# Second attention of a decoder layer: when the value products, the projections and the copies are issued within a unit of sixteen steps

## The reference

```
q = _heads(x @ Wq + bq); k = _heads(x @ Wk + bk); v = _heads(x @ Wv + bv)      # 16 heads of 16
att = einsum('bhqd,bhkd->bhqk', q, k) * scale, -inf above the diagonal
y = einsum('bhqk,bhkd->bhqd', softmax(att), v)
qc = _heads(x @ Wcq + bcq); kc = _heads(cross_input @ Wck + bck); vc = _heads(cross_input @ Wcv + bcv)
attc = einsum('bhqd,bhkd->bhqk', qc, kc) * scale
y = y + einsum('bhqk,bhkd->bhqd', softmax(attc), vc)
return y @ Wp + bp
```

## Time and profile before

| | |
|---|---|
| time, median of 3 runs | 1344.24 us (1342.76 to 1344.56) |
| the profiled execution | 1347.11 us, its span 1345.4 us |
| PE busy in the span | 1190.8 us, 89% |
| DVE busy | 913.5 us, 68% |
| ACT busy | 830.3 us, 62% |
| POOL busy | 479.5 us, 36% |
| first maximum and last score of the second attention | 617.3 and 1018.2 us |

### The profile page before, as it was taken

One profiled execution on the slowest core, in us unless ns is written; L12 is line 12 of the kernel. 1 busy time (PEld: TensorE's weight loads), 2 busy tenths in 40 slices (PEclk: granted clock), 3 DMA queues, 4 the chain that ended last, 5 costly groups with the idle time before them and its releaser, 6 DMA issues. The chain is left out here.

```text
span 1345.4 us, 25018 instructions
## 1 busy us (share of the span) xinstructions
PE 1190.8 (89%) x8862; PEld 552.4 (41%) x8862; DVE 913.5 (68%) x2337; ACT 830.3 (62%) x1584; POOL 479.5 (36%) x511
## 2 busy tenths in 40 slices
PE   6699999999999999375888888888888369999998
PEld 2244444444444443261222232232224336666666
DVE  3777777777777777435788887878841755756564
ACT  3466666666666666450577777677773465666663
POOL 0267888877888888420112111111220000000000
PEclk9999999999999999696799999999997679999999
DMA  7544222222222221202121211212100082332100
GB/s 220 156 98 103 54 57 50 49 51 57 54 57 52 49 49 24 89 8 84 46 69 49 68 52 47 68 46 60 44 2 1 2 313 78 127 125 80 64 16 17
DMA packets 75954, 91.98 MB, mean 68 GB/s; under 512 B 12242, under 2 KB 67538, under 8 KB 75798
## 3 DMA queue, kind: packets, MB, share of 16 engines
q1 hardware_dynamic: 74806, 90.25, 23.9%
q0 software_dynamic: 1024, 0.13, 0.1%
HBM read 54.36 MB, written 10.68 MB: 48 GB/s over the span
## 5 line engine op out<-in xcount | busy, mean ns | idle before, releaser
L1023 DVE TENSOR_REDUCE a_mx<-a_m 128x1 f32<-128x512 f32 (+3 forms) x512 | 269.0, 584 | 74.6 <-PE a_m L829 62.8
L960 ACT ACTIVATE a_pt<-a_s 128x512 f32<-128x512 f32 (+3 forms) x512 | 235.5, 515 | 88.4 <-PE a_s L857 85.1
L449 ACT ACTIVATE a_pt<-a_s 128x512 f32<-128x512 f32 x256 | 149.4, 597 | 164.3 <-DVE a_s L544 135.8
L829 PE MATMUL a_m<-a_k,a_q 48*128 48x512 f16 (+3 forms) x512 | 131.0, 362 | 53.9 <-DVE a_mx L1023 44.2
L537 DVE CUSTOM_DVE_ANT_0 a_junk<-a_m,a_rtile 128x512 f16<-128x512 f32 x256 | 167.3, 687 | 2.0 <-issue 2.0
L604 POOL TENSOR_TENSOR a_ps<-a_ps,a_pt 128x512 f32<-128x512 f32 x128 | 159.9, 1272 | 1.4 <-ACT a_pt L449 1.4
L333 PE MATMUL a_o<-a_pt,a_v 128*64 128x512 f32 x512 | 139.0, 621 | 0.1
L829 PEld LDWEIGHTS a_m<-a_k,a_q 48*128 48x128 f16 x512 | 36.2, 94 | 202.1 <-DVE a_mx L1023 160.7
L870 PE MATMUL a_o<-a_pt,a_v 128*17 128x512 f32 (+3 forms) x1024 | 119.1, 538 | 0.0
L544 DVE TENSOR_TENSOR a_s<-a_s,a_near 128x218 f32<-128x218 f32 (+1 forms) x256 | 108.0, 433 | 15.5 <-PE a_s L324 12.9
L857 PE MATMUL a_s<-a_q,a_k 49*128 49x512 f16 (+3 forms) x512 | 114.4, 352 | 3.3 <-ACT a_pt L960 3.1
(11 more groups left out here) (208 smaller groups left out, 2430.8 us busy)
## 6 DMA issues: line engine op xcount, KB each, us to landing
a_q<-a_nat SPq DMA_DIRECT2D x192, 64.0 KB
a_k<-a_nat SPq DMA_DIRECT2D x192, 64.0 KB
ex_raw<-in_Wa SPq DMA_DIRECT2D x12, 1024.0 KB, 4.9
ex_raw<-in_Wb SPq DMA_DIRECT2D x12, 1024.0 KB, 7.1
halves<-a_natc SPq DMA_DIRECT2D x32, 128.0 KB, 2.4
halves<-a_nat SPq DMA_DIRECT2D x16, 256.0 KB, 2.1
a_q<-halves SPq DMA_DIRECT2D x32, 128.0 KB, 2.7
a_k<-halves SPq DMA_DIRECT2D x32, 128.0 KB, 2.8
```

The source lines that it names most:

```text
L449: act.activation(pt[:, n % RING, ::-1], bank_s[j % 2][:, :], ACT.Exp, scale=SC1 / QS).then_inc(sm["act_s"], 1)
L829: mm[h] = pe.matmul(bank_m[j % 3][:, 0:keys], q[u % 3][o:o + ROW_M, pair, x, qb * P:(qb + 1) * P], k[u % 3][o:o + ROW_M, pair, x, 0:keys], ...
L960: act.activation(pt[g % 4][:, h, first:], bank_s[(32 * u + j) % 3][:, first:], ACT.Exp, scale=SC2 / QS).then_inc(sm["act_s"], 1)
L1023: dve.tensor_reduce(mx[u % 2][:, qb, to:to + 1], bank_m[j % 3][:, 0:keys], AX.X, ALU.max).then_inc(sm["dve_b"], 1)
```

## The change

The table of steps changes in five places, and the two chunks of a projection are issued in one step instead of two. In steps of the period (all counted as above):

| | before | after |
|---|---|---|
| cross projection, PE | 4 and 5 | 4 |
| self projection, PE | 11 and 12 | 10 |
| high and low half of self, ACT and DVE | 12 and 13 | 11 and 12 |
| value products, PE | 10, 12, 14, 0, 2, 4, 6, 8 | 11, 13, 15, 1, 3, 5, 7, 9 |
| copies of `bank_o`, ACT | 1 and 9 | 2 and 10 |
| turn back, PE, and weigh, DVE | 8 and 15 | 8 and 14 |

Rows (step 1) and the high and low halves of cross (5 and 6) stay.

```diff
-        CROSS, SELF, MAX, ROWS_AT, SCORE, VALUE, COPY, TURN, ADD = -12, -5, 16, 33, 38, 42, (49, 57), (56, 63), 64
+        CROSS, SELF, MAX, ROWS_AT, SCORE, VALUE, COPY, TURN, ADD = -12, -6, 16, 33, 38, 43, (50, 58), (56, 62), 64
...
-            def project_self(u, c):
+            def project_self(u):
                 b, g = divmod(u, GROUPS)
-                if c == 0 and u > 3:
+                if u > 3:
                     pe.wait_ge(sm["dve_y"], 2 * u - 7)
-                elif c == 0:
+                else:
                     pe.wait_ge(sm["dve_cross"], u + 1)
...
+                product(bank_a[:, :], [(whi[:, o:o + P], wlo[:, o:o + P], xhi[:, c, xs], xlo[:, c, xs])
+                                       for c, o in enumerate(at)]).then_inc(sm["pe_self"], 1)
...
-                u, i = unit_at(n, CROSS, 2)
-                if u is not None and (u % 2 == 0 or i == 0):
-                    project_cross(u, i)
-                u, i = unit_at(n, SELF, 2)
+                u, i = unit_at(n, CROSS)
                 if u is not None:
-                    project_self(u, i)
+                    project_cross(u)
+                u, i = unit_at(n, SELF)
+                if u is not None:
+                    project_self(u)
```

More of the change, by code:

```diff
@@ L766, in tensor, with product @@
             pe.wait_ge(sm["cst"], 6 * DMA)
-            def product(out, parts, first=True, last=True):
+            def product(out, parts):
                 steps = [s for wh, wl, xh, xl in parts for s in ((wh, xh), (wl, xh), (wh, xl))]
                 for i, (w, x) in enumerate(steps):
-                    mm = pe.matmul(out, w, x, start=first and i == 0, stop=last and i == len(steps) - 1)
+                    mm = pe.matmul(out, w, x, start=i == 0, stop=i == len(steps) - 1)
                 return mm
@@ L790, in tensor, with project_cross @@
             pe.wait_ge(sm["cleared"], 1)
-            def project_self(u, c):
+            def project_self(u):
                 b, g = divmod(u, GROUPS)
-                if c == 0 and u > 3:
+                if u > 3:
                     pe.wait_ge(sm["dve_y"], 2 * u - 7)
-                elif c == 0:
+                else:
                     pe.wait_ge(sm["dve_cross"], u + 1)
[L798 to L803, removed]
+                xs, at = slice(b * S, (b + 1) * S), [QK_AT + (c * GROUPS + g) * P for c in range(KC)]
+                product(bank_a[:, :], [(whi[:, o:o + P], wlo[:, o:o + P], xhi[:, c, xs], xlo[:, c, xs])
+                                       for c, o in enumerate(at)]).then_inc(sm["pe_self"], 1)
+            def project_cross(u):
                 b, g = divmod(u, GROUPS)
-                if c == 0 and u > 2:
+                if u > 2:
                     pe.wait_ge(sm["act_rows"], u - 2)
-                elif c == 0 and u > 0:
+                elif u > 0:
                     pe.wait_ge(sm["dve_self"], u)
@@ L811, in project_cross @@
                 if u % 2 == 0:
-                    o, moving = CQ_AT + c * C + g // 2 * P, (xhi[:, c, xs], xlo[:, c, xs])
-                else:
[L814 to L818, removed]
+                    at = [CQ_AT + c * C + g // 2 * P for c in range(KC)]
+                    parts = [(whi[:, o:o + P], wlo[:, o:o + P], xhi[:, c, xs], xlo[:, c, xs]) for c, o in enumerate(at)]
+                else:
+                    o = CK_AT + g // 2 * P
+                    parts = [(whi[:, o:o + P], wlo[:, o:o + P], chi[:, xs], clo[:, xs])]
+                product(bank_a[:, :], parts).then_inc(sm["pe_cross"], 1)
             def maximum(u, i):
```

## The result

The changed kernel takes 1351.84 us (median of 15 runs), the kernel before 1343.67 in the same session: the ratio is 1.0055, 95% interval 1.0037 to 1.0072. It is slower by 0.55%, where I had forecast 0.26% faster. Its runs spread from 1342.68 to 1355.56 us, and **they lie on a line with TensorE's mean granted clock**: the run of 1342.68 had 0.954, those of 1346.5 to 1348.7 had 0.947 to 0.951, the six slowest, 1353.8 to 1355.6, had 0.941 or 0.942. The kernel before, timed 118 more times beside the experiments, lies on nearly the same line: 0.954 is its median clock, with a median of 1342 us there, and its 11 runs at 0.947 take 1346.4 to 1348.2, where the changed kernel's two take 1348.4 and 1350.5.

A forecast was written before the change was run, and what follows sets the result against it. It took PE and DVE, neither full, to lose time waiting for each other in turn. 3.9 us gained in the steady part, 0.4 lost at the start, 0 at the end: 1344.24 - 3.5 = 1340.7 us, range 1331 to 1349.

The forecast's parts named there:

- The steady part: Units with maxima and scores side by side: 23.35 us in the mean against 23.62, 3.9 us gained over 14.6 units.
- The cross maxima of 5 to those of 11: Steps 5 to 10 of a unit: 8.77 us against 8.63, as DVE's low half and weigh stand in the way.
- from there to the first score of 0: Steps 11 to 0 of a unit: 7.59 us against 7.55, bounded by DVE before and after, nothing gained.
- ACT bounds steps 0 to 3: Start of a unit: PE, 0.9 to 1.1 us early, waits for ACT before the second score of step 3.
- the other signs on the timeline: Causal maxima start together in steps 6 and 8; maxima of 14 and 0 wait for DVE; ACT without gap.
- a pair of units: Steady part: two units take 46.7 us instead of 47.2; below 45.5 or above 47.5 the prediction is wrong.
- The start: First 22 steps, DVE the limit: merged projections hold up the maxima, 0.4 us lost, bounds -1 to +1.5.
- The end: Last 22 steps, without maxima: order kept but for one value group, between -0.5 and +0.5 us, taken as 0.
- rival 3: PE's waits gathered before a score of step 3 lower TensorE's clock in each unit: 1354 us, or 1347; chance 0.20.

The follow-up runs named there:

- n2: Kernel before with only the projections of the first three units merged and moved as in the change: 1345.01 us, ratio 1.0020 to the kernel before.
- g3: Changed kernel with the projections of the first three units in two steps again (old start): 1344.05 us, ratio 1.0016 to the kernel before.
- n1: Kernel before with values, copies, turns and weighs of the last two units alone at the changed steps: 1348.93 us, ratio 1.0053.
- k1: Kernel before with products that nothing reads added before the first maximum and in the steps without scores at the start: 1341.94 us, ratio 0.9992.
- e2: Kernel before with only the projections merged into one step, values, copies and turns as before: 1369.85 us, ratio 1.0205.
- g2: Changed kernel with first three units' projections in two steps and last two units' values, copies and turns at old steps: 1344.84 us, ratio 1.0013 to before.
- g1: Changed kernel with values, copies, turns and weighs of the last two units at their old steps: 1347.64 us, ratio 1.0032 to the kernel before.
- v1: Changed kernel with old start, old order in the last two units, unread products in the other units' step 3 wait: 1351.26 us, ratio 1.0067 to before.

## Why the prediction was wrong

**The steady part: right in mechanism, 0.15 us off in size.** The forecast was 23.02 and 23.68 us for odd and even units. They take 23.18 and 23.82. The cross maxima of 5 to those of 11 take 822.61 - 813.75 = 8.86 (forecast 8.77), from there to the first score of 0 it is 7.74 (7.59): DVE begins its chain a little later than I had it. ACT bounds steps 0 to 3 as forecast, and the other signs on the timeline came as well; a pair of units takes 47.0 us, not 46.7. The clock is 0.99 over ten steady units, as in the kernel before, from one dip in each trace. The gain is thus 0.11 us a unit, not 0.27: of the 3.9 us for 14.6 units, 1.6 remain, and one dip of the clock, as in the unit of 24.71 us in the trace of after, takes back 1.5 of it.

**The start: this term was too small.** I had put +0.4 us, with +1.5 as the bound. In all seven traces with merged projections at an unfilled start it takes 25.0 to 25.6 us, in the others 23.2 to 23.7: +1.8 in the mean. Its price for the whole is 2.5 us in n2 and 6.0 by g3, so it reaches beyond the start itself, and how is not shown: of n2's 12 runs 4 are at 0.953 or above, of the kernel before 84 of 118.

**The end: this is the step that failed most plainly.** "In the last 22, without maxima, PE and ACT keep their order but for one value group: between -0.5 and +0.5, taken as 0." At full clock it is +0.9 (27.3 against 26.4), in n1's trace +3.7, and in the two of the changed kernel some 8.8 above the 26.4 of k1 and n2, because TensorE is cold for part of it. I had walked through the steady part link by link, and had not done so for the end, where the wait for ACT that I found myself stands alone, without maxima around it. The sum priced no change of the clock in either place; only rival 3 did.

**Rival 3 was the right one, in the wrong place.** I had priced it for the steady part and given it 0.20, because the steady windows of before are at 1.00. The rows that spoke for it were those of the end, 0.50 over 16 us with PE busy for 15.36 of them: they said that this stretch is near the edge. I had also read the earlier trace rows as if the clock swung only where DVE bounds the loop; that holds for its first two rows, but near the end there are no maxima and PE waits for ACT. What I had against the rival, that PE's share of busy time does not fall, was true and no argument.

The Trainium skill's rule ("TensorE: Matmul & The Clock Gate", section "A second HAM failure mode: psum-queue depth-cycling"), that brief idle times between groups of products that cycle through PSUM banks let the clock go back and forth, is borne out by e2 (0.91 over ten units, no wait of PE for DVE there above 0.9 us) and by the end, and not by the steady part of either kernel, which cycles through the same banks with waits of up to 0.5 and 0.9 us and keeps 0.99. Nor do these runs say which waits do it: behind one of 0.97 us the clock fell in the changed kernel and not in g3, behind one of 0.45 it fell in g2 and not in g1.

## What to carry to other kernels

A wait that is moved is not neutral even when it costs no time of its own. Here the change made the steady part some 1.6 us faster, dips apart, and lost 8.2 us on the whole, since in most runs TensorE was longer at 1.2 GHz at the loop's two ends; products that nothing reads, put into a wait of each unit, gave back 4 us, and 8.9 together with the old start. Walk through the first and the last units of a pipelined loop as carefully as through its steady part, and read the granted clock by stage beforehand: here the stages below 1.00 were those where a small change of order had a large price. Where runs spread by 1%, compare them at the same clock; one trace of each kernel can show two different draws. Before a single wait is blamed for a fall of the clock, look for a trace that has the same wait and no fall.

## What was unexpected of the hardware

The granted clock is low although PE counts as busy: 0.50 in the last stage with 15.36 of 16 us busy, 0.55 over 38 us in v1 with 34.67 busy. At 1.2 GHz its products take nearly twice as long (a value group of 512 columns 1.91 us instead of 1.05), so its share of busy time is high because it is slow, and says nothing of how it came there. And TensorE at full clock at the start (20.26 us instead of 23.7) hardly shortened the whole: the next unit ran at 0.66 and took back 1.6 of the 3.5 us. The same products with the same waits ran at 2.4 GHz in one trace and at 1.2 in another (g1 and g2, g3 and after), so the order alone does not fix the clock. Why v1 and g2 have 34 us at 1.2 GHz at their end was not settled.
